# Four-layer graph network, 32 graphs: statistics taken two tiles at a time, a diagonal scaled on VectorE, bias sums on GpSimd, orders anew

## The reference

```python
def _layernorm(x, axis=-1, eps=1e-5):
    m = jnp.mean(x, axis=axis, keepdims=True)
    v = jnp.var(x, axis=axis, keepdims=True)
    return (x - m) / jnp.sqrt(v + eps)

# layer 0: pair scores, softmax over axis 1, sigmoid
e = (x @ a_i)[:, :, None] + (x @ a_j)[:, None, :]      # mean and var over all pairs, times adj
h = sigmoid(einsum('bij,bjd->bid', softmax(leaky(e), axis=1), x))
# layer 1: attention masked by adj, layernorm, then a two-layer MLP on (1+eps)*h + A@h
x_gin = einsum('bmk,ko->bmo', z, W2) + b2
return relu(x_gin + h_gat)
# layer 2: A is one softmax for all graphs, M the identity
out = einsum('ij,bjg->big', A * M, h0) + einsum('ij,bjg->big', A * (1.0 - M), h1)
return out + bias[None, None, :]
# layer 3: attention masked by adj with loops, elu
return elu(einsum('bij,bjo->bio', attn, h))

x = _layernorm(x + layer(x))      # after each of the four
```

## Time and profile before

| what | value |
|---|---|
| median of three runs | 1194.18 us (1192.84 to 1195.81) |
| the profiled execution: its span, first to last instruction | 1188.6 us |
| what the three runs have around a span of that length | 4.2 to 7.2 us |
| TensorE (matmul) busy | 1103.5 us, 93% |
| VectorE busy | 1055.8 us, 89% |
| ScalarE busy | 964.7 us, 81% |
| GpSimd busy | 594.6 us, 50% |

### The profile page before, as it was taken

How to read it: one execution, slowest core, us unless ns; L and a number is a source line. 1 busy time by engine, 2 the same in 40 slices (tenths; PEclk the granted TensorE clock), 3 DMA queues, 4 the chain that set the end, 5 groups by cost and what they waited for, 6 DMA issues and landing times.

```text
span 1188.6 us, 28920 instructions
## 1 busy us (share of the span) xinstructions
PE 1103.5 (93%) x7752; PEld 907.9 (76%) x7752; DVE 1055.8 (89%) x3894; ACT 964.7 (81%) x2453; POOL 594.6 (50%) x1250
## 2 busy tenths in 40 slices
PE   4779999999999999999999999999999999999964
PEld 3457777888777888887778888877778888788743
DVE  6887999999999999999999999999999899997642
ACT  3566888888888888888888889888888898888753
POOL 4243435555564555556555555555545554553422
...
GB/s 76 19 36 19 27 28 46 31 31 22 22 35 35 35 35 35 26 28 17 35 35 35 35 35 26 35 9 35 35 35 35 29 37 30 17 46 10 28 9 19
DMA packets 59478, 36.17 MB, mean 30 GB/s; under 512 B 3872, under 2 KB 54816, under 8 KB 59424
## 3 DMA queue, kind: packets, MB, share of 16 engines
...
...
## 4 chain that ended last, share of the span: by engine, by line
PE 58%; POOL 10%; issue 9%; DVE 5%; ACT 2%; DMA 1%; POOLq 0%; SPq 0%; ACTq 0%; DVEq 0%
PE ps L965 14%; PE ps L893 7%; PE ps L949 6%; PE ps L982 4%; PE ps L1025 4%; PE ps L934 4%; PE ps L744 4%; PE ps L737 3%; POOL rirA L559 2%; PE ps L1014 2%; PE ps L880 2%; PE ps L1043 2%; PE ps L1042 2%; PE ps L919 1%; DMA xA<-in_x_dram 1%
## 5 line engine op out<-in xcount | busy, mean ns | idle before, releaser
L965 PE MATMUL ps<-hE,pTE 128*128 128x128 f32 x1024 | 131.0, 277 | 0.2
L982 PE MATMUL ps<-gin_j,hgat 128*128 128x512 f32 x256 | 124.4, 610 | 3.0 <-DVE gin_j L1495 1.8
L965 PE MATMUL ps<-hB,pTB 128*128 128x128 f32 x1024 | 125.3, 275 | 0.7 <-DVE pTB L1626 0.6
L893 PE MATMUL ps<-xsA,pA 128*128 128x128 f32 x1024 | 124.4, 275 | 0.0
L965 PEld LDWEIGHTS ps<-hE,pTE 128*128 128x128 f32 x1024 | 122.8, 193 | 0.9 <-issue 0.6
L1025 PE MATMUL ps<-att_j,xD 128*128 128x512 f32 x256 | 122.3, 601 | 0.8 <-ACT xD L2207 0.8
L965 PEld LDWEIGHTS ps<-hB,pTB 128*128 128x128 f32 x1024 | 119.4, 192 | 1.4 <-DVE pTB L1626 1.1
L893 PEld LDWEIGHTS ps<-xsA,pA 128*128 128x128 f32 x1024 | 119.4, 192 | 0.4 <-issue 0.3
L2250 ACT ACTIVATE pA<-vA,nmA,rirA 128x512 f32<-128x512 f32 x128 | 107.0, 845 | 6.3 <-DVE vA L1683 5.3
L2312 ACT ACTIVATE pE<-wE,mnE 128x512 f32<-128x512 f32 x128 | 92.4, 723 | 20.9 <-DVE mnE L1613 20.8
L1595 DVE SCALAR_TENSOR_TENSOR wE<-ps,hE,y2E 128x512 f32<-128x512 f32 x128 | 92.1, 739 | 13.8 <-ACT y2E L2282 13.7
...
## 6 DMA issues: line engine op xcount, KB each, us to landing
...
```

The costliest lines, as they stand in the source:

```text
L893: last = mm(at("aggA")[:, i * P:(i + 1) * P], pA[:, j, i * P:(i + 1) * P], xsA[:, j], start=(j == 0), stop=(j == NT - 1))
L965: last = mm(at("agg" + n)[:, i * P:(i + 1) * P], att[n]["pT"][:, i, j], att[n]["h"][:, j, 0:P], start=(j == 0), stop=(j == NT - 1))
L982: last = mm(at("gin"), hgat[:, j], gin_j[:, j], start=(j == 0), stop=(j == NT - 1))
```

## The change

1. `bn_stats` now runs on two tiles at a time. The tiles are interleaved in its access pattern, element by element, so that the instruction's even and odd statistics are those of the one and of the other tile. Twelve instructions stand in a turn where 24 stood, and all 24 `bn_aggr` are gone. GpSimd forms variance plus epsilon from the raw sum; for B VectorE does it in one small instruction (`ve_B`).
2. The diagonal: TensorE transposes xD, and VectorE multiplies by the diagonal, spread once in the setup over all partitions, while it copies from PSUM (`diag_D`). ScalarE's `copy_xTD` is gone.
3. The biases of `x2_C` and `out_D` are added on GpSimd to what is summed later (`bias_C`, `bias_D`); the two matmuls that spread them are gone. The bias rows that are split into bf16 parts in the setup are 258 wide in place of 514.
4. GpSimd also keeps xE less one (`minus_E`), so that `y_E` is a plain sum.
5. `scale_xA` reads xrA, and the load of xA no longer waits for it.
6. All lists, the PSUM bank table and the loop boundaries are new. `dots_A` and `mean_A` stand at the end of VectorE's turn, one graph earlier; `x2_C` stands in the turn of `zT_C` (delay 3, was 4).

```diff
-                    if k == "B":
-                        pool.wait_ge(s["zzB"], g.now)
-                        pool.wait_ge(s["aggr_B"], g.now)
-                    else:
-                        pool.wait_ge(s["stats_" + k], g.now)
-                    eps = zzB[:] if k == "B" else consts[:, 2:3].to_broadcast([P, NT])
-                    pool.tensor_tensor(L["ve"][:], L["mv"][:, :, 1], eps, ALU.add).then_inc(s["ve_" + k], 1)
-                    pool.wait_ge(s["ve_" + k], g.now)
+                    pool.wait_ge(s["ve_B" if k == "B" else "bn_" + k], g.now)
...
+                    if k != "B":
+                        pool.tensor_scalar(L["ve"][:], L["m2"], 1.0 / P, LN_EPS, ALU.mult, ALU.add).then_inc(s["ve_" + k], 1)
+                        pool.wait_ge(s["ve_" + k], g.now)
...
+            def bias_C(g):
...
+                pool.wait_ge(s["applied_B"], g.now)
+                pool.wait_ge(s["qC_ready"], g.last)
+                pool.tensor_tensor(hgb[:], hgat[:], bias_2, ALU.add).then_inc(s["hgb_ready"], 1)
+
+            def bias_D(g):
...
+                pool.wait_ge(s["applied_C"], g.now)
+                pool.wait_ge(s["y_D"], g.last)
+                pool.tensor_tensor(xDb[:], xD[:], bias_l2, ALU.add).then_inc(s["xDb_ready"], 1)
+
+            def minus_E(g):
+                pool.wait_ge(s["applied_D"], g.now)
+                pool.wait_ge(s["y_E"], g.last)
+                pool.tensor_tensor(flat(xEm[:]), flat(xE[:]), consts[:, 3:4].to_broadcast([P, N]), ALU.add).then_inc(s["xEm_ready"], 1)
...
-                features("x2", zT, w2_sb[:], bias_2).then_inc(s["x2C_in_psum"], 1)
+                features("x2", zT, w2_sb[:]).then_inc(s["x2C_in_psum"], 1)
...
-                for i in range(NT):
-                    last = mm(at("xTD")[:, i * P:(i + 1) * P], xD[:, i], dia[:, i], start=True, stop=True)
-                last.then_inc(s["xD_scaled"], 1)
+                transpose("xTD", xD).then_inc(s["xD_transposed"], 1)
...
-                mm(tiles(at("outD")), onesb[:], bias_l2, start=True, stop=False, skip_group_check=True)
...
+        def two_tiles(src, half):
+
+            return src[:, half * 2 * P:(half + 1) * 2 * P].rearrange("p (u d) -> p d u", u=2)
...
-                for i in range(NT):
-                    last = v.bn_stats(ln["B"]["st"][:, i], at("aggB")[:, i * P:(i + 1) * P])
+                for half in range(NT // 2):
+                    last = v.bn_stats(ln["B"]["st"][:, half], two_tiles(at("aggB"), half))
...
+                v.scalar_tensor_tensor(L["ve"][:], L["m2"], 1.0 / P, zzB[:], ALU.mult, ALU.add).then_inc(s["ve_B"], 1)
...
+            def diag_D(g):
...
+                dve.wait_ge(s["xD_transposed"], g.now)
+                dve.wait_ge(s["outD_ready"], g.last)
+                v.tensor_tensor(xTdD[:], at("xTD"), diaT, ALU.mult).then_inc(s["xTdD_ready"], 1)
...
-                v.scalar_tensor_tensor(ln["E"]["y"][:], y1E[:], -1.0, xE[:], ALU.add, ALU.add).then_inc(s["y_E"], 1)
+                v.tensor_tensor(ln["E"]["y"][:], y1E[:], xEm[:], ALU.add).then_inc(s["y_E"], 1)
...
-                    last = a.activation(xsA[:, j], xA[:, j], ACT.Copy, scale=rzA[:, j:j + 1])
+                    last = a.activation(xsA[:, j], xrA[:, j], ACT.Copy, scale=rzA[:, j:j + 1])
...
-                t.run(scale_xD, 4)
...
+                t.run(transpose_xD, 4)
```

More of the change, by code:

```diff
@@ new lines, in fill @@
+                t.graph(3, gain_B)
+                t.graph(5, sumsq_A)
+                t.graph(3, offset_B)
+                t.graph(1, L_E0)
+                t.graph(4, bn_A)
+                t.graph(1, M_E0, L_E1, L_E2, M_E1, L_E3, M_E2)
+                t.graph(5, v_A0)
+                t.graph(2, diag_D)
+                t.graph(5, v_A1)
+                t.graph(1, M_E3)
+                t.graph(5, v_A2, v_A3, lrelu_A0, max_A)
+                t.graph(3, bn_Z)
+                t.graph(5, lrelu_A1, offset_A)
@@ L1918, in turn @@
+                t.graph(1, recip_E)
+                t.graph(4, mult_B3, bn_B, zz_B, ve_B)
+                t.graph(6, dots_A0, dots_A1)
+                t.graph(1, y1_E)
+                t.graph(6, mean_A)
+                t.graph(1, y_E)
             def turn(t):
-                t.run(dots_A0, 1)
-                t.run(dots_A1, 1)
                 t.run(bn_E, 6)
-                t.run(mean_A, 1)
+                t.run(gain_B, 3)
+                t.run(sumsq_A, 1)
+                t.run(offset_B, 3)
@@ new lines, in drain @@
+                t.graph(GRAPHS - 4, y_A)
+                t.graph(GRAPHS - 3, sumsq_A)
+                t.graph(GRAPHS - 4, bn_A)
+                t.graph(GRAPHS - 7, L_E0)
+                t.graph(GRAPHS - 8, y_E)
+                t.graph(GRAPHS - 7, M_E0, L_E1, M_E1, L_E2, L_E3)
+                t.graph(GRAPHS - 8, bn_E)
+                t.graph(GRAPHS - 3, v_A0)
+                t.graph(GRAPHS - 7, M_E2, M_E3)
+                t.graph(GRAPHS - 3, v_A1, v_A2)
+                t.graph(GRAPHS - 6, diag_D)
@@ L2155, in _ @@
+                t.graph(GRAPHS - 1, recip_E)
+                t.graph(GRAPHS - 2, bn_E)
+                t.graph(GRAPHS - 1, y1_E, y_E, bn_E)
             turns(dve, fill, turn, drain)
@@ L2336, in copy_zT @@
                 a.activation(zT[:], at("zT"), ACT.Relu, scale=mlp_gb[:, 0:1], bias=mlp_gb[:, 1:2]).then_inc(s["zT_ready"], 1)
-            def copy_xTD(g):
-                act.wait_ge(s["xD_scaled"], g.now)
-                act.wait_ge(s["outD_ready"], g.last)
-                a.copy(xTdD[:], at("xTD")).then_inc(s["xTdD_ready"], 1)
             def copy_axD(g):
```

1544 lines of the change are left out of this document (779 added, 765 removed), and 6 rows, old and new, of the table IN_BANK.

## The result

The changed kernel takes 1186.8 us (median of five runs, 1184.5 to 1187.4), the kernel before 1193.1 (median of five, 1190.6 to 1195.8): a ratio of 0.9947, 95% interval 0.9932 to 0.9963. It is faster, by 6 us where 26 were forecast, and lies 0.8 us above the end of the range. All times in this document are medians of runs in the fast state; one run of e9 (1388.7 us, granted clock 0.75) and one of the kernel before in the same group as e9 to e12 (1607.8 us, 0.65) were slow and are left out. The profiled execution has a span of 1185.0 us against 1188.6.

What follows compares the result with a forecast made beforehand. TensorE (32.45 us) and VectorE (32.2) bound together; with 0.35 of coupling the turn is 32.8, saving 18.7 us over 22 turns and 8 at the ends: span 1161.9, plus 5.6 around it, predicted 1168 us, range 1160 to 1177 (chance 0.52).

Steps and rivals of the forecast that it cites:

- TensorE's work: TensorE in a turn: two bias matmuls (0.44) and the cheaper diagonal (0.46) save 0.90 us; alone it turns in 32.45.
- The stall ahead of t_B: TensorE's third stall in a turn, 0.3 us: should go, since two groups of transposes now stand ahead of t_B.
- The statistics: VectorE's norms: no bn_aggr saves 1.8 us a turn, paired bn_stats at 0.66 us a pair save 0.7.
- third rival: The twelve bn_stats: interleaved reading is slow, 1.6 us more a turn at one and a half times the slope, 1208; chance 0.10.
- VectorE's wait for xA: VectorE's 0.32 us wait in each turn goes, its load being issued some 25 us ahead of its reader.
- The price of the sums: GpSimd's three 512-column sums, 1.2 us each, hold VectorE's two-input instructions for 1.0 us a turn; bounds 0 and 3.0.
- the coupling: TensorE 32.45 and VectorE 32.2, in one ring, don't meet without loss: 0.35 us added, 32.8 us a turn.
- circle: One ring through both engines: `squares_A` on TensorE, VectorE from `sumsq_A` to B's first masked product, TensorE's aggregation of B.
- second rival: Each GpSimd sum holds VectorE 0.6 us or more: VectorE 33.0, with the coupling 33.3 a turn, 1182 us; chance 0.13.
- the ends: Start and end outside the loop, 448 us with ten graphs' work: 0.8 us a graph, 8 us saved; bounds -18 and +3.
- 0.3 a layer: In the chain at the end, `bn_aggr` leaves, saving 0.3 us a layer; part of the ends' 8 us.
- What bounds the kernel: The loop before: TensorE 32.45 us unstalled, VectorE 32.97, neither comfortably ahead; a change pays only as far as both shorten.

Runs made afterwards that it cites:

- e9: e3 with the old statistics put back, each bn_aggr group one instruction behind its bn_stats: 1245.1 us.
- e12: e3 with VectorE's product of the transposed xD and the diagonal cut to 4 of 512 columns: 1169.9 us.
- e1: The changed kernel with its three GpSimd sums cut to 4 of 512 columns, waits and order kept: 1156.5 us.
- e6: The changed kernel with SyncE's load of xA put ahead of keep_xB in its queue: 1185.1 us.
- e10: e3 with SyncE's load of xA also put ahead of keep_xB: 1166.0 us.
- e16: The changed kernel with only the bias of C sum moved, ahead of norm_E in GpSimd's turn; minus_E stays: 1168.4 us.
- e3: The changed kernel with two GpSimd sums moved in the loop turn, minus_E behind square_A and bias_C ahead of norm_E: 1165.8 us.
- e15: The kernel before with the new interleaved statistics alone, its orders, matmuls and sums unchanged: 1193.3 us, ratio 0.9980 to 1.0010.
- e13: e3 with the old statistics put back, bn_aggr near its bn_stats and C's ahead of B's bn_stats: 1220.5 us.

## Why the prediction was right in direction and wrong in size

**TensorE's work: right.** 0.90 us less was forecast, 1.07 measured (33.06 to 31.99). The stall ahead of t_B went, the one ahead of `rows_A` stayed. TensorE's own turn, 32.45 forecast, is 32.51 in e1. Its parts are less good than their sum: the trace before has 33.06 us of work and 0.68 of gap, where the prediction had 32.45 and 1.2.

**The statistics: right in size.** A pair of 256 takes 0.68 us of room (613.64 to 614.32, and 625.62 to 626.30 from PSUM), 0.66 forecast; the third rival is refuted. The Trainium skill's remark (Vector Engine (DVE) Microarchitecture Reference, section 5.2, Measured stream behaviour on trn2) that a one-source stream alternating between two regions 16 KiB apart runs at the full rate agrees with these rows, in which the two regions are tiles 512 bytes apart.

**VectorE's wait for xA: wrong, without effect.** The load doesn't wait for ScalarE any more, but stands behind keep_xB in SyncE's queue, which waits for y_C (606.50, then 607.61), and the dots wait 0.64 us. The diff shows the new semaphore; only the queue's order shows what is now last. e6 and e10 put the worth of it at nothing clear of noise.

**The price of the sums: right in total, in part by luck.** 1.09 and 1.49 us long against 1.2; 1.04 us a turn held against 1.0. But the prediction had built its 1.0 from about 0.4 us for each of three sums, and the trace has 0.87, 0.17 and nothing. The Trainium skill's rule (SBUF — State Buffer, section Who interferes with whom), that whichever starts first keeps the port pair to its end, agrees to the letter: 0.09 us of lead for hgb made the mask 1.55 us long, 0.13 of lead for the mask in e16 made the sum 1.47.

**The step that failed is the coupling.** "I add 0.35 us, about a third of VectorE's lost 1.0." I had a circle written down in the sentence before, and then compared two totals, VectorE's 32.2 and TensorE's 32.45, as though slack elsewhere on VectorE could take up a hold inside the circle. What the runs show in its place: VectorE's slack (0.80 us for agg_B, 0.64 for xA, 0.53 for y2B) stands outside its part of the circle, from y2B to the first masked product of B, and what is held inside passes whole, 1.02 us of turn for 1.04 of hold between e1 and the changed kernel. e3 and e16, whose masks are held for 0.0 and 0.25 us, have 32.63 and 32.77. The circle as I had written it was also wrong in its first half: from varA to y2B it runs over GpSimd and ScalarE, not over VectorE's own work. By its turn the second rival was nearly right, 33.3 against 33.53, for the wrong cause: not the sum over VectorE's work but two holds of 0.87 and 0.17 us in the wrong place. Of the 23 us by which the span missed its forecast, 16 are 22 x (33.53 - 32.8).

**The other 7 us are the ends.** What lies outside 22 turns was to be 440 us (448 less 8, with bounds -18 and +3) and is 447.3. The kernel before had 446.3, not 448, since its mean turn is 33.74 and not 33.65; that is 2 us of the forecast's 8. e3, where no mask is held in the loop, has the same ends (445.4), but e1, which has no whole sum anywhere, has 1155.5 - 22 x 32.51 = 440.3. So the ends that I forecast are there once the sums are gone, and the term that I left out is what the sums cost in the first and last turns, some 5 to 7 us by this difference; which of them does it there, no run shows. e15 shows that the new statistics alone leave the ends at 445.8: the "0.3 a layer" that I took from the chain at the end was not there either. What the new orders would have given apart from the rest was not measured.

**What bounds the kernel: half right.** I wrote that before neither engine was ahead and that a change pays only as far as both become shorter. e15 says that VectorE was not a bound: 2.2 us of work taken off it changed nothing. The 32.97 us that I gave it were the turn less two named waits; its busy time was 32.05 us a turn (569.9 in 600) and its idle time 1.7. VectorE's cut mattered all the same, since with TensorE at 32.0 the old statistics have a turn 1.2 us longer even in the best of three placings (e13).
